# A fused two-norm block on one Trainium2 core: the first norm's turn by VectorE squares and DMAs, the second norm's scaling on ScalarE

## The reference, cut to what matters

```python
x = x + attn(_layernorm(x))     # "first norm"
x = x + ffn(_layernorm(x))      # "second norm"

def attn(x):                    # D_INNER 512, D_STATE 16, D_CONV 4
    xp, z = split(x @ w_in)     # 256 -> 2 x 512
    xc = silu(causal_conv4(xp) + conv_b)          # depthwise over time
    h = h * 0.9 + 0.1 * (xt @ w_B); y = h @ w_C   # scan over the tokens of a sequence
    return (y * silu(z)) @ w_out                  # 512 -> 256

def ffn(x):                     # 8 experts, the top 2 by the sequence's first token
    idx = top_k(x[:, 0, :] @ Wr + br, 2)
    h = gelu(x @ W1[idx] + b1[idx])
    return sum(h @ W2[idx] + b2[idx]) / 2
```

## Time and profile before

| | us |
|---|---|
| median of 3 runs | 563.06 |
| the profiled execution's own time | 561.46 |
| its span | 559.6 |
| TensorE matmul busy | 532.1 (95%) |
| VectorE busy | 459.4 (82%) |
| ScalarE busy | 374.3 (67%) |
| GpSimd busy | 341.6 (61%) |

### The profile page before, as it was taken

One profiled execution on the slowest core, in us unless ns is written; L12 is line 12 of the kernel. 1 busy time (PEld: TensorE's weight loads), 2 busy tenths in 40 slices (PEclk: granted clock), 3 DMA queues, 4 the chain that ended last, 5 costly groups with the idle time before them and its releaser, 6 DMA issues. The chain is left out here.

```text
span 559.6 us, 9988 instructions
## 1 busy us (share of the span) xinstructions
PE 532.1 (95%) x3168; PEld 463.6 (83%) x3168; DVE 459.4 (82%) x935; ACT 374.3 (67%) x626; POOL 341.6 (61%) x346
## 2 busy tenths in 40 slices
PE   0879899999999999999999999999999999999897
PEld 0668688888888888988888888888889888898886
DVE  2779899968988789978999689996899789794793
ACT  2766577676866776776677668667776766776343
POOL 3657659464885458683585637944587745654570
PEclk9989999999999999999999999999999999999999
DMA  6791100312020120302103120111203002020211
GB/s 172 195 332 39 39 1 14 101 39 75 0 89 23 37 75 0 112 0 68 44 0 112 37 75 0 56 56 37 75 0 94 19 19 57 0 76 0 75 39 40
DMA packets 35397, 32.54 MB, mean 58 GB/s; under 512 B 5426, under 2 KB 34610, under 8 KB 35250
## 3 DMA queue, kind: packets, MB, share of 16 engines
q1 hardware_dynamic: 33266, 31.48, 17.7%
q10 hardware_dynamic: 2112, 0.83, 0.7%
HBM read 23.91 MB, written 8.39 MB: 58 GB/s over the span
## 5 line engine op out<-in xcount | busy, mean ns | idle before, releaser
L561 DVE SCALAR_TENSOR_TENSOR conv<-blk,tap_w,conv 128x512 f32<-128x512 f32 x192 | 129.7, 742 | 10.8 <-ACT conv L398 9.6
L303 POOL TENSOR_TENSOR y_lo<-gate,y_hi 128x512 fp32r<-128x512 f32 x64 | 81.0, 1297 | 70.7 <-ACT y_hi L355 70.7
L274 POOL TENSOR_TENSOR xc_lo<-conv,xc_hi 128x512 fp32r<-128x512 f32 x64 | 80.9, 1279 | 47.7 <-ACT xc_hi L355 47.7
L719 PE MATMUL blk<-xn_hi,w_in_hi 128*128 128x512 f32 x256 | 103.9, 406 | 1.7 <-DVE conv L561 1.7
L720 PE MATMUL blk<-xn_hi,w_in_lo 128*128 128x512 f32 x256 | 101.9, 398 | 0.0
L724 PE MATMUL blk<-xn_lo,w_in_hi 128*128 128x512 f32 x256 | 80.8, 397 | 0.0
L496 DVE TENSOR_TENSOR hid_lo<-hid,hid_hi 128x512 fp32r<-128x512 f32 x64 | 50.4, 807 | 34.1 <-ACT hid_hi L355 34.1
L766 PE MATMUL tok<-w_out_hi,y_hi 128*128 128x256 f32 x256 | 72.3, 282 | 0.0
L766 PE MATMUL tok<-w_hi,hid_hi 128*128 128x256 f32 x256 | 72.2, 282 | 0.0
L768 PE MATMUL tok<-w_hi,hid_lo 128*128 128x256 f32 x256 | 71.6, 280 | 0.0
L768 PE MATMUL tok<-w_out_hi,y_lo 128*128 128x256 f32 x256 | 71.5, 279 | 0.0
(11 more groups left out here) (79 smaller groups left out, 1250.1 us busy)
## 6 DMA issues: line engine op xcount, KB each, us to landing
x_in<-in_L_attn_x SPq DMA_DIRECT2D x16, 512.0 KB, 3.4
x_mid<-in_L_attn_x SPq DMA_DIRECT2D x32, 256.0 KB, 2.8
out<-x_mid SPq DMA_DIRECT2D x32, 256.0 KB, 2.7
w_all<-in_L_ffn_W SPq DMA_DIRECT2D x2, 2048.0 KB, 12.3
b_all<-in_L_ffn_b SPq DMA_DIRECT2D x1, 1024.0 KB, 14.8
gate<-in_L_attn_w_in ACTq DMA_DIRECT2D x1, 512.0 KB, 6.2
gate<-in_L_attn_w_in SPq DMA_DIRECT2D x1, 512.0 KB, 7.5
hid<-in_L_attn_w_out SPq DMA_DIRECT2D x1, 512.0 KB, 9.2
```

The source lines that it names most:

```text
L274: nc.gpsimd.tensor_tensor(xc_lo[:, j, :], conv[:, j, 0:CH], xc_hi[:, j, :].bitcast(F32), ALU.subtract).then_inc(xc_lo_set, 1)
L303: nc.gpsimd.tensor_tensor(y_lo[:, j, :], gate[:, j, :], y_hi[:, j, :].bitcast(F32), ALU.subtract).then_inc(y_lo_set, 1)
L561: nc.vector.scalar_tensor_tensor(cols, blk[j][:], tap_w[:, j, t:t + 1], cols, ALU.mult, ALU.add).then_inc(tap_added, 1)
L719: mm(dst, whi(k), his(k), start=(k == 0), stop=False)
```

## The change

For every chunk but the first, the first norm's result no longer goes through TensorE:

1. GpSimd's `norm1` writes its four tiles interleaved in blocks of 32 channels (`[P, 8, 4, 32]`).
2. VectorE turns the whole chunk in place in one instruction, in squares of 32x32 (`turn_squares`). That leaves the squares on the wrong partitions.
3. SyncE issues 16 DMAs (`permute`), each of 32 partitions by 2 runs of 512 bytes, from `normed1` to the new tensor `turned_sb`.
4. ScalarE makes the hi part from `turned_sb` after the gelus (it stood before them), and GpSimd makes the lo part (VectorE did), between its last `split_conv` and `choose_b2`/`add_b2`.

The second norm's scaling moves from VectorE (4 instructions with mean and inverse deviation) to ScalarE (4 instructions `x * rstd + shift`), after `state_hi` and before `y_his`; VectorE only computes `shift` (128x4). SyncE's list is reordered: permute, two stores, two refills, fetch.

```diff
+            def permute(c):
+                sp.wait_ge(squares_set, c)
+                for g in range(QUADS):
+                    for a in range(QUADS):
+                        sp.dma_start(turned_sb[a * SQ:(a + 1) * SQ, :, g * P:(g + 1) * P],
+                                     squares_k[g * SQ:(g + 1) * SQ, :, a, :]).then_inc(permuted, 16)
...
             fetch(2)
+            permute(1)
...
             def norm1(c):
-                if not (isinstance(c, int) and c == 0):
-                    pool.wait_ge(turned1, c * KD)
+                first = isinstance(c, int) and c == 0
+                if isinstance(c, int) and c == 1:
+                    pool.wait_ge(turned1, KD)
+                elif not first:
+                    pool.wait_ge(permuted, (c - 1) * QUADS * QUADS * 16)
...
+            def turn1_lo(c):
+                for k in range(KD):
+                    pool.wait_ge(t1_hi, c * KD + k + 1)
+                    nc.gpsimd.tensor_tensor(by_tile(xn1_lo, k), natural(turned_sb, k),
+                                            by_tile(xn1_hi, k).bitcast(F32), ALU.subtract).then_inc(t1_lo, 1)
...
+                    act.wait_ge(permuted, c * QUADS * QUADS * 16)
+                    for k in range(KD):
+                        hi(by_tile(xn1_hi, k), natural(turned_sb, k)).then_inc(t1_hi, 1)
...
+            def norm2(o, q):
+                act.wait_ge(shift_set, o + 1)
+                for n in range(TT):
+                    ins = nc.scalar.activation(normed2[:, n, :], x_mid[:, q, n, :], ACT.Identity, bias=shift[:, n:n + 1],
+                                               scale=rstd2[:, n:n + 1])
+                ins.then_inc(norm2_ready, 1)
...
-                if has_next(s, 1):
-                    turn1_hi(a + 1)
                 if has_ffn(s):
                     if has_attn(s):
                         warm(ACT.Gelu)
                     gelus(f, q, half - 1)
+                if has_next(s, 1):
+                    turn1_hi(a + 1)
                 if has_attn(s):
                     state_hi(a, q)
+                if has_out(s):
+                    norm2(o, 1 - q)
...
+            def turn_squares(c):
+                dve.wait_ge(norm1_ready, c + 1)
+                nc.vector.transpose(squares, squares).then_inc(squares_set, 1)
...
                 if has_ffn(s):
                     turn2_lo(f)
+                if has_next(s, 1) and not first:
+                    turn_squares(a + 1)
                 if has_attn(s):
                     taps(a, 0)
+                if first:
+                    turn_squares(1)
```

More of the change, by code:

```diff
@@ L156, in build_block, with natural, by_tile @@
         raw_c = hid[:, JF - 1, :]
+        tiles_first = normed1[:].rearrange("p b n i -> p (b n i)").rearrange("p (n d) -> p n d", n=TT)
+        squares = normed1[:].rearrange("p b n i -> p (b n i)")
+        squares_k = normed1[:].rearrange("p b n i -> p b (n i)").rearrange("p (k a) c -> p k a c", k=KD)
+        def natural(t, k):
+            return t[:, k, :].rearrange("p (g n j) -> p n g j", g=QUADS, n=TT)
+        def by_tile(t, k):
+            return t[:, k, :].rearrange("p (n g j) -> p n g j", g=QUADS, n=TT)
         LAST = NC - 1
@@ L229, in _ @@
             fetch(3)
+            permute(2)
             fetch(4)
@@ L308, in add_b2 @@
                     pool.wait_ge(b2_set, seq * 2 + 2)
-                pool.wait_ge(norm2_ready, f * 2 + 2)
+                pool.wait_ge(norm2_ready, f + 1)
                 for n in range(TT):
@@ L341, in step @@
                     split_conv(a, (3,))
+                if has_next(s, 1):
+                    turn1_lo(a + 1)
                 if has_ffn(s):
@@ L378, in turn1_hi @@
             def turn1_hi(c):
-                for k in range(KD):
-                    act.wait_ge(turned1, c * KD + k + 1)
-                    hi(xn1_hi[:, k, :], turn[k][:]).then_inc(t1_hi, 1)
+                if isinstance(c, int) and c == 0:
+                    for k in range(KD):
+                        act.wait_ge(turned1, k + 1)
+                        hi(xn1_hi[:, k, :], turn[k][:]).then_inc(t1_hi, 1)
+                else:
+                    act.wait_ge(permuted, c * QUADS * QUADS * 16)
+                    for k in range(KD):
+                        hi(by_tile(xn1_hi, k), natural(turned_sb, k)).then_inc(t1_hi, 1)
             def turn2_hi(o):
@@ L535, in stats2, with shift2, turn1_lo_first @@
                 nc.vector.tensor_scalar(var_eps2[:], mean_var2[:, :, 1], EPS, None, ALU.add).then_inc(stats2_ready, 1)
-            def norm2(o, q, h):
+            def shift2(o):
                 dve.wait_ge(rstd2_set, o + 1)
[L539 to L544, removed]
+                nc.vector.scalar_tensor_tensor(shift[:], mean_var2[:, :, 0], -1.0, rstd2[:], ALU.mult,
+                                               ALU.mult).then_inc(shift_set, 1)
+            def turn1_lo_first():
                 for k in range(KD):
-                    dve.wait_ge(t1_hi, c * KD + k + 1)
+                    dve.wait_ge(t1_hi, k + 1)
                     lo(xn1_lo[:, k, :], turn[k][:], xn1_hi[:, k, :]).then_inc(t1_lo, 1)
+            def turn_squares(c):
+                dve.wait_ge(norm1_ready, c + 1)
+                nc.vector.transpose(squares, squares).then_inc(squares_set, 1)
             def turn2_lo(o):
@@ L699, in turns, with turns1 @@
                     ins.then_inc(sem_out, 1)
[L701 to L705, removed]
-            def turns2(o):
-                if has_next(o, 2):
-                    pe.wait_ge(t1_lo, (o + 3) * KD)
-                pe.wait_ge(norm2_ready, o * 2 + 2)
+            def turns1():
+                pe.wait_ge(norm1_ready, 1)
+                turns(tiles_first, turned1)
+            def turns2(o):
+                if isinstance(o, int) and o == 0:
+                    pe.wait_ge(t1_lo, KD)
+                else:
+                    pe.wait_ge(t2_lo, o * KD)
+                pe.wait_ge(norm2_ready, o + 1)
                 turns(normed2, turned2)
```

35 lines of the change are left out of this document (22 added, 13 removed).

## The result

| | before | after |
|---|---|---|
| median of the runs, us | 562.14 (561.84 to 563.33, 5 runs) | 567.04 (566.39 to 569.27, 5 runs) |
| the profiled execution's own time | 561.46 | 569.27 |
| its span | 559.6 | 567.1 |
| TensorE matmul busy | 532.1 (95%) | 527.8 (93%) |
| VectorE / ScalarE / GpSimd busy | 82 / 67 / 61% | 76 / 71 / 65% |

After over before is 1.0087, 95% interval 1.006 to 1.0113: slower by 4.9 us. The forecast was 567.0: +3.9 us on the 563.06 of three runs, where the five runs now give 562.14. The two profiled executions are 7.8 us apart, since the one of after was the slowest of its five runs. So terms read from the traces are set against 7.8, and the kernels are compared by their medians.

A forecast was written before the change was run, and what follows sets the result against it. From step 2 on TensorE's list was taken to set the step's length. -11.4 saved, +9.0 GpSimd stalls and +6.3 start gave +3.9 us on 563.06, so 567.0 us; 8-in-10 range 557.5 to 578.

The forecast's parts named there:

- TensorE's saving: Steps 2 to 14: without the eight transposes and the gap behind them, 0.88 us a step, -11.4 us.
- GpSimd late in even steps: `y_lo` ready 1.5 us behind TensorE's need in `out_proj`, six times, +9.0 us; odd steps do not stall.
- E: The end of `z`, where the transposes begin; times with a plus are counted from it.
- The port of VectorE and GpSimd: GpSimd's `xn_lo` beside VectorE's `hid_lo` and `state_mix`: 0.3 us for contention; 1.0 by the skill's rule.
- The squares: VectorE's 128x1024 transpose, taken as 1.4 us (bounds 1.1 and 2.9), hidden in the steady state.
- Four scalings: The second norm's scalings on ScalarE, 0.5 us each, 2 us between `state_hi` and the table load.
- The DMAs: Sixteen issues at 0.51 us, landing about 3 us later: hidden in the steady state, not at the start.
- The start: Steps 0 and 1: ScalarE waits for the DMAs, squares stand ahead of the taps, +6.3 us together.
- GpSimd does not become late: Rival, chance 0.22: no stall in `out_proj`, only the saving and starting cost remain, -5.1 us, 558.0 us.
- the block-wise operands cost more: Rival, chance 0.12: block-wise operands or VectorE port slow GpSimd between `hid_hi` and `y_lo`; sum +17.1, 580.2 us.
- the DMAs are slow: Rival, chance 0.09: 0.82 us an issue and 4.0 to land make the start 17.9; sum +15.5, 578.6 us.

The follow-up runs named there:

- lo_dve: The changed kernel with the lo part of the first norm back on VectorE, between `state_lo` and `ys`: 559.45 us, 0.994 of before.
- b2_early: The changed kernel with GpSimd's `choose_b2` moved ahead of `split_conv`: 559.11 us, 0.9919 of before.
- b2_first: The changed kernel with GpSimd's `choose_b2` put ahead of `turn1_lo`: 567.6 us, 1.0094 of before.
- norm2_act: The kernel before with only the second norm's scaling moved to ScalarE: 562.47 us, 0.9996 of before.
- by_pe3: The changed kernel with chunks 1 and 2 turned by TensorE as before the change: 558.69 us, 0.9933 of before.
- pe3_lo_dve: The changed kernel with chunks 1 and 2 turned by TensorE and the first norm's lo part on VectorE: 553.23 us, 0.9813 of before.

## Why the prediction was right

The mechanism was right: the saving, six stalls for `y_lo` and a longer start. The number is in part luck. The forecast time came out within 0.1 us, but +3.9 stands against a measured +4.9, and the median before is 0.9 lower than the one it was added to. Inside the sum the start was 3.6 us too small. Half of that came back in the steady state, in blocks for which the prediction had no term, and much of the rest is not seen in the medians, which are 4.9 apart where the two traces are 7.8.

- **TensorE's saving, -11.4.** In the trace the transposes are gone, and `up` takes 5.58 instead of 5.69. That holds in the changed kernel, which has no new wait for VectorE in the steady state. Measured alone in another version it was 7.0 to 9.5 (expected 11.4), since about 2 us of it went to waits for VectorE, which there has the lo part to do as well.
- **GpSimd late in even steps, +9.0.** Right, and nearly in every item (from `E`): `xn_lo` starts at +7.86 (I had +7.9), takes 2.72 (2.8), `choose_b2` and its gaps 2.3 (1.97), `x_mid` 2.83 (2.82), `pow1` and `norm1` 3.38 (3.59), `y_lo` ends at +24.08 (+24.2). The stall was 1.6 to 1.7 a step for 1.5, 9.6 to 10 for 9.0. lo_dve and b2_early take it away and win 7.6 and 7.9. Odd steps do not stall, as said.
- **The port of VectorE and GpSimd.** I had put 0.3 us for contention. For the changed kernel that was enough, because the idle time of GpSimd keeps the two apart: the mean of a `hid_lo` fell from 807 ns before to 689 ns. The Trainium skill, "SBUF — State Buffer", section "SBUF: two separate sides", has the shared port locked for a whole instruction by a VectorE operation with two SBUF inputs, against a GpSimd one that reads SBUF. The rows differ from a full lock: in b2_first `hid_lo` ran 3.78 us beside about 3 us of GpSimd work and lost 1.28, and GpSimd's own lost about 0.3 in `b_sel` and 0.7 in `xn_lo`. The direction of the rule holds, and the overlap cost b2_first its whole gain. That the port is what the two contend for is the page's account; the runs show only that they slow each other.
- **VectorE.** The squares took 1.24 each, where I took 1.4. The Trainium skill, "VectorE: DVE Perf Modes", section "The three transpose paths", has 311 ns for a bf16 128x128; the estimate of 2.5 made from it is twice the measured time, and the measured number decides. In the steady state they were hidden.
- **ScalarE.** Four scalings took 2.06 (I took 2.0), and norm2_act shows no cost of them.
- **The DMAs.** Hidden in the steady state, as said: outside the start no `xn_hi` waits for one. An issue took 0.645 us (10.33 / 16), where I took 0.51 from SP's rows. ACT's 0.82 was the other bound, and the truth is about in the middle. Landing was 1.9 in the median, less than SP's 2.8.
- **The start, +6.3.** This is the mis-sized term: it was 9.9 in the trace (9.05 at `up` of step 2, which has one saved turn in front of it), and by_pe3 wins 8.4 by taking it away. Step 0 was +3.3 for +2.3, since 15 issues at 0.645 are 2.0 more than at 0.51, less 1.0 for the shorter landing and square. Step 1 was +7.7 for +6.3: 1.0 of the difference is step 0's (it came down to `norm1`, done at 51.0 where I had 49.9), the shorter square gives 0.15 back, and 0.6 more passed between the last tap and `state_mix`. The other 2.2 us are a kind of cost that the prediction did not have: the granted clock fell to 0.50 in step 1, behind the wait of 3.33, where in the kernel before it stayed at 1.00.
- **What made up for it.** From `up` of step 2 to the last steps the trace is 3.3 us shorter, where the sum had 1.6 (12 x 0.88 less six stalls of 1.5). Twelve turns less and six stalls more are 12 x 0.88 - 6 x 1.61 = 0.9 of it (`out_proj` 5.65 before, 7.26 after). Another 1.0 is in thirteen blocks of `down`, whose first 36 matmuls took 4.24 to 4.41 before and 4.20 now, where `hid_lo` is no longer disturbed; that this is the reason I only argue. The rest is hundredths in every other block: `z` 5.57 for 5.60, the even `out_proj` 5.70 for 5.76, `xp` 5.76 for 5.78. norm2_act has nearly the same hundredths (`z` 5.57, `out_proj` 5.60 and 5.71) with all the transposes in place. So they belong to the second norm's move or to that one profile of the kernel before, and not to the turn.
- **The two executions.** The profile of after has 1.7 us of lower clock at its end. Its `out_proj` of step 16 takes 7.23 us there, with no wait in it, and 5.52 before. In the other traces it is 7.07 to 7.27 in seven and 5.71 in two (by_pe3 and b2_first); norm2_act, which has the old turn, is among the seven. I count it for neither side. It does enter the 4.9 us: the kernel before took 564.1 to 564.9 us in its twelve executions beside the experiments whose mean granted clock was 0.990, and 561.6 to 562.9 in those at 0.996; the changed kernel took 566.4 to 567.0 at 0.990 and 568.7 and 569.3 at 0.984. So at a like mean clock it is about 2 us slower. The rest of the 4.9 goes with the clock, partly that of the start, behind the longer wait, and partly this.

Of the rivals, "GpSimd does not become late" fell on the 18 waits, "the block-wise operands cost more" on `normed` at 2.16 for four (2.18 before), and "the DMAs are slow" on 0.645 and 1.9, though it had the right direction for the start.

Not tried: the squares behind the taps in step 1, which could keep more of the DMA path at the start.

## What to carry to other kernels

An instruction saved on the engine that sets the pace is worth its time only until the next engine is late, so list that next engine's work item by item up to its next hand-over, as was done here for GpSimd; 1.5 us over is 1.5 us lost, each time. If GpSimd's list has idle time, look at what VectorE does in it before filling it: the same two instructions cost 8.5 us or not by where they stood. A longer path (here 16 DMAs, 12 us in all) that is hidden in the loop is paid in full in the first steps, and there the old path can be kept.

## What the runs showed of the hardware

- A wait can cost more than itself. In step 1 of the changed kernel the granted clock was 0.50 (1.2 GHz) up to about 74.3, though TensorE was busy again from 69.6; four matmuls took 2.08 us instead of 1.19, and the work up to `xp` 1.6 us more.
- How long the wait was does not alone decide it. The eleven traces have 22 waits ahead of `state_out` in steps 0 and 1. Behind the ten of 3.06 us and more the clock fell to 0.50 each time. Behind the twelve of 2.75 to 2.93 it fell six times (the kernel before in step 0, pe3_lo_dve in both steps) and stayed at 1.00 six times (the kernel before in step 1, norm2_act in both). At the end of the kernel, behind a wait of 2.3 us, it fell in eight of eleven. So a difference of 2 us between two single executions can be clock alone.
- A 128x1024 float32 turn in squares on VectorE took 1.24 us (15 instances), less than the one subtraction of the same shape (1.43 in the earlier trace rows).
- A 32 KB transfer within SBUF took SyncE 0.645 us to issue and 1.9 us to land.
- Operands in blocks of 32 elements cost GpSimd nothing: 2.16 for four `normed` and 1.27 for an `xn_lo`, as for contiguous ones.
